# Silu evaluated on ScalarE in one group a tile, z projected a tile ahead, convolution taps folded into the projection's weights

## What is computed

```python
def silu(v): return v * sigmoid(v)
x_d, z = split(einsum('btm,im->bti', x, W_in))       # 512 channels each
xc = depthwise causal conv of x_d, 4 taps, + conv_b
x_d = silu(xc)
ssm_in = x_d @ W_x.T                                  # dt_raw (1), B (16), C (16)
delta = softplus(dt_raw * W_dt + b_dt)
for each token:                                       # the scan, h is [512, 16]
    h = exp(delta * A) * h + delta * B * x_d
    y = (h * C).sum(over the 16 states)
y = (y + D * x_d) * silu(z)
x = y @ W_out.T                                       # residual and layer norm follow
# experts: h = silu(t @ wg.T) * (t @ wu.T); out += weight * (h @ wd.T)
```

## Time and profile before

| | |
|---|---|
| time, median of 3 runs | 1134.51 us (1130.51 to 1134.89) |
| the profiled execution | 1135.04 us, its span 1133.2 us |
| busy share of the span | PE 85%, DVE 82%, POOL 70%, PEld 64%, ACT 60% |
| mean granted TensorE clock | 0.949 |
| start, to the first scan | 46.4 us |
| mixer stage, 11 tiles | 46.4 to 774 us |
| between the stages | 774 to 801 us |
| expert stage | 801 to about 1105 us, then the last sums to 1133 us |

### The profile page before, as it was taken

How to read it: one execution, slowest core, us unless ns; L and a number is a source line. 1 busy time by engine, 2 the same in 40 slices (tenths; PEclk the granted TensorE clock), 3 DMA queues, 4 the chain that set the end, 5 groups by cost and what they waited for, 6 DMA issues and landing times.

```text
span 1133.2 us, 16674 instructions
## 1 busy us (share of the span) xinstructions
PE 964.0 (85%) x4563; PEld 725.6 (64%) x4563; DVE 928.9 (82%) x1821; ACT 681.6 (60%) x1802; POOL 788.1 (70%) x839
## 2 busy tenths in 40 slices
PE   5698889988798888989978896866599999999990
PEld 5575666656566566666756663534388888878880
DVE  3589999999999999999999999896244677767774
ACT  3685675757567575666757657541266666666661
POOL 2244478878788787888878888787501676767775
PEclk8999999999999999999999999878799999999996
DMA  4599500201111020111202010058566898889883
GB/s 150 176 327 325 160 24 24 62 15 59 38 50 52 19 80 18 54 42 33 74 15 59 10 53 29 28 210 354 146 188 179 251 269 263 260 259 277 265 265 108
DMA packets 104474, 149.21 MB, mean 132 GB/s; under 512 B 14111, under 2 KB 91359, under 8 KB 104127
## 3 DMA queue, kind: packets, MB, share of 16 engines
q1 hardware_dynamic: 87487, 106.35, 29.3%
q0 software_dynamic: 16896, 41.80, 13.0%
HBM read 71.28 MB, written 76.82 MB: 131 GB/s over the span
## 4 chain that ended last, share of the span: by engine, by line
POOL 26%; PE 26%; issue 18%; DVE 17%; ACT 7%; DMA 3%; SPq 1%; POOLq 0%; DVEq 0%; ACTq 0%
POOL arena L630 11%; PE BC L1007 11%; DVE arena L1408 9%; POOL pool_dram L618 6%; PE Y L1001 3%; PE F L1021 3%; PE K L1021 3%; DMA mixer_own<-pool_dram 3%; DVE arena L1420 2%; ACT D L1118 2%; PE Y L842 2%; POOL arena L637 1%; PE D L1013 1%; ACT arena L1069 1%; POOL gat L686 1%
## 5 line engine op out<-in xcount | busy, mean ns | idle before, releaser
L1408 DVE TENSOR_TENSOR_SCAN arena<-D,arena 128x444 f32<-128x444 f32 (+1 forms) x352 | 351.1, 1037 | 12.4 <-ACT D L1118 8.3
L842 PE MATMUL Y<-arena,ident 128*128 128x444 f32 (+1 forms) x704 | 303.3, 559 | 1.6 <-DVE arena L1420 1.6
L686 POOL DMA_INDIRECT gat<-y_dram,slot_all x176 | 173.5, 986 | 127.5 <-DMA y_dram<-mixer_own 72.5
L618 POOL DMA_INDIRECT pool_dram<-hrow,slot_of x176 | 175.4, 997 | 45.3 <-issue 38.1
L630 POOL TENSOR_TENSOR arena<-mixer_own,arena 128x888 f32<-128x888 f32 (+1 forms) x90 | 163.9, 1823 | 53.2 <-ACT arena L1106 51.6
L1118 ACT ACTIVATE D<-mixer_own,aneg 128x216 f32<-128x216 f32 (+1 forms) x384 | 148.5, 427 | 82.4 <-DVE arena L1408 82.2
L1420 DVE TENSOR_TENSOR arena<-arena,BC 128x888 f32<-128x888 f32 (+1 forms) x176 | 184.8, 1050 | 5.4
L1007 PE MATMUL BC<-arena,xt 128*128 x716 | 185.3, 382 | 0.0
L630 POOL TENSOR_TENSOR arena<-arena 128x888 f32<-128x888 f32 x75 | 143.4, 1913 | 53.8 <-ACT arena L1106 52.9
L842 PEld LDWEIGHTS Y<-arena,ident 128*128 128x128 f32 x704 | 127.0, 199 | 74.8 <-issue 70.0
L1118 ACT ACTIVATE D<-arena,aneg 128x216 f32<-128x216 f32 x320 | 126.8, 437 | 73.1 <-DVE arena L1408 73.1
(11 more groups left out here) (232 smaller groups left out, 1644.1 us busy)
## 6 DMA issues: line engine op xcount, KB each, us to landing
mixer_own<-pool_dram SPq DMA_DIRECT2D x179, 144.0 KB, 3.6
y_dram<-mixer_own SPq DMA_DIRECT2D x179, 128.0 KB
pool_dram<-filler SPq DMA_DIRECT2D x5, 4176.0 KB, 31.4
arena<-in_experts_dram SPq DMA_DIRECT2D x1, 7680.0 KB, 22.8
arena<-in_x_dram SPq DMA_DIRECT2D x10, 648.0 KB, 4.0
pool_dram<-filler SPq DMA_DIRECT2D x1, 4896.0 KB, 36.1
arena<-in_experts_dram SPq DMA_DIRECT2D x1, 4608.0 KB, 17.5
pool_dram<-hrow,slot_of POOLq DMA_INDIRECT x176, 2.7
```

What stands on the lines that cost most here:

```text
L618: nc.gpsimd.indirect_dma_start(out=pool_rows, out_offset=bass.IndirectOffsetOnAxis(ap=slot_of[q][0:r, b, k:k + 1], axis=0), in_=hrow[q][0: ...
L686: nc.gpsimd.indirect_dma_start(out=gat[0:r, k, b, :], out_offset=None, in_=y_rows[0:(blocks_by(t) - k) * P, :], in_offset=bass.IndirectOff ...
L842: mm = nc.tensor.matmul(Y[j][:, 0:w], ident[:], read[g % 3][:, j * w:(j + 1) * w], start=(s == 0), stop=(s == STATES - 1), skip_group_chec ...
L1408: nc.vector.tensor_tensor_scan(state[g % 2][:, lo:hi], D[b][:, 0:hi - lo], drive[g % DRIVES][:, lo:hi], 0.0, ALU.mult, ALU.add).then_inc(s ...
```

## The change

- **Silu on ScalarE.** The function Silu is evaluated directly. `take_conv` (step 1) copies the first half of the convolution raw into x2, `silu_conv` (step 8) evaluates the second half out of bank F and the first half in SBUF. `silu_z` (step 8) evaluates all of z, 888 elements. The shared expert's gate moves to step 8. The set with Ln and exp is loaded again right behind this group. VectorE's four products of 444 a tile and one of the two of `shared_expert` and of `hidden` are gone.
- **z a tile ahead.** `project_z` now takes tile n = i+1 in steps 12 and 14, and ScalarE copies it to `z_raw` (`take_z`). It took tile i before. `add_tokens` waits for `z_taken` instead of VectorE's last product.
- **Taps in the weights.** `inw4` holds the projection's weights times each tap (set up once by VectorE, 8 products of 512 elements). `convolve(n, c, k)` multiplies the tokens themselves: 32 + 4 matmuls a tile, and no `project_x`, no `copy_x_d`. The tap weights are loaded broadcast over the 128 partitions.
- **Softplus moved.** `softplus_small` goes from step 13 to step 12, `softplus_large` from behind the read-out of step 13 to ahead of it. `shared_expert` goes from the end of step 8 to between scan and read-out of step 9.

```diff
-inw_x = carve(KM * DI).rearrange("p (k d) -> p k d", k=KM)
-diag_w = carve(KI * TAPS * P).rearrange("p (c a d) -> p c a d", c=KI, a=TAPS)
-x_d = carve(2 * N)
+inw4 = carve(KM * TAPS * DI).rearrange("p (k a d) -> p k a d", k=KM, a=TAPS)
 xw = carve(KI * SPLIT).rearrange("p (c a r) -> p c a r", c=KI, a=3)
 dtw = carve(KI * P).rearrange("p (c d) -> p c d", c=KI)
-half_tanh, soft, small, series = (carve(KI * N) for _ in range(4))
+logs, soft, small, series = (carve(KI * N) for _ in range(4))
...
+inw_x = arena[:, at_drive:at_drive + KM * DI].rearrange("p (k d) -> p k d", k=KM)
+convw = arena[:, at_drive + 2 * KI * N:at_drive + 2 * KI * N + TAPS * DI].rearrange("p (a d) -> p a d", a=TAPS)
...
-tanh_z, z2, gated, delta_even, du_even = (mixer_own[:, n] for n in range(5))
+z_raw, z2, gated, delta_even, du_even = (mixer_own[:, n] for n in range(5))
...
-CONV_LOADS = [(inw_x, w_in_x), (convw[:], conv_w),
+CONV_LOADS = [(inw_x, w_in_x), (convw, conv_w.broadcast_to([P, TAPS, DI])),
...
-    def project_x(n, b):
-
-        if b == 0:
+    def convolve(n, c, k):
+        if c == 0 and k == 0:
             pe.wait_ge(h0_done, n + 1)
-        else:
-            pe.wait_ge(x2_done, 2 * n + 1)
-        if n == 0:
-            pe.wait_ge(conv_in, 16 * len(CONV_LOADS))
+        if n == 0 and c == 0:
+            pe.wait_ge(inw4_done, k + 1)
+        if c == 2 and k == 0:
+            pe.wait_ge(conv_taken, n + 1)
         w = width(n)
-        for c in range(2):
-            for k in range(KM):
-                at = 2 * b + c
...
+        to = F[:, (c % 2) * w:(c % 2 + 1) * w]
         for back in range(TAPS):
-            nc.tensor.matmul(to.rearrange("p (a t) -> p a t", t=TOKENS)[:, :, back:], diag_w[:, c, TAPS - 1 - back, :],
-                             of[:, :, 0:TOKENS - back], start=(back == 0), stop=False, skip_group_check=True)
-        if n == 0 and c == 0:
...
+            nc.tensor.matmul(to.rearrange("p (a t) -> p a t", t=TOKENS)[:, :, back:], inw4[:, k, TAPS - 1 - back, c * P:(c + 1) * P],
+                             h0[n % 3][:, k, 0:images(n), 0:TOKENS - back], start=(k == 0 and back == 0), stop=False,
+                             skip_group_check=True)
+        if k == KM - 1:
+            if n == 0 and c == 0:
+                pe.wait_ge(bias_split, 4)
+                pe.wait_ge(one_rows_step, 4)
+            nc.tensor.matmul(to, bias_rows[:, c * P:(c + 1) * P], one_rows[:, 0:w], start=False,
+                             stop=True, skip_group_check=True).then_inc(conv_done, 1)
...
-    def project_z(i, b):
+    def project_z(n, b):
+
         if b == 1:
-            pe.wait_ge(z2_done, 2 * i + 1)
+            pe.wait_ge(z_taken, 2 * n + 1)
         else:
-            if i > 0:
-                pe.wait_ge(rank_taken, i)
-            else:
+            if n > 1:
+                pe.wait_ge(rank_taken, n - 1)
+            if n == 0:
                 pe.wait_ge(mixer_in, 16 * len(MIXER_LOADS))
-            if i + 1 < TILES:
-                pe.wait_ge(bc_split, SPLITS * (i + 1) + 2)
-        w = width(i)
+            pe.wait_ge(bc_split, SPLITS * n + 2)
+        w = width(n)
...
-        pe.wait_ge(z2_done, 2 * t + 2)
+        if t + 1 < TILES:
+            pe.wait_ge(z_taken, 2 * t + 4)
+        else:
+            pe.wait_ge(rank_taken, t)
...
-            convolve(n, 1)
+            for k in range(KM):
+                convolve(n, 1, k)
...
-        if front and s == 4:
-            project_x(n, 1)
-        if front and s == 6:
-            convolve(n, 2)
+        if front and s in (4, 5):
+            convolve(n, 2, s - 4)
...
-        if front and s == 8:
-            convolve(n, 3)
+        if front and s in (7, 8):
+            convolve(n, 3, s - 7)
...
-        if mix and s in (12, 14):
-            project_z(i, (s - 12) // 2)
+        if front and s in (12, 14):
+            project_z(n, (s - 12) // 2)
         if i + 2 < TILES:
             if s in (11, 13):
                 project_patches(i + 2, (s - 11) // 2)
-            if s == 14:
-                project_x(i + 2, 0)
-            if s == 15:
-                convolve(i + 2, 0)
+            if s in (14, 15):
+                convolve(i + 2, 0, s - 14)
...
-    def copy_x_d(n, b):
-        act.wait_ge(x_d_done, 2 * n + b + 1)
-        if 2 * n + b > 0:
...
+    def take_conv(n):
+
+        act.wait_ge(conv_done, KI * n + 2)
+        if n > 1:
+            act.wait_ge(x_added, n - 1)
+            act.wait_ge(du_done, n - 1)
+        nc.scalar.activation(cut(x2[n % 2], n)[:, 0:2, :], pair(F, n), ACT.Copy).then_inc(conv_taken, 1)
+
+    def silu_conv(n):
+        act.wait_ge(conv_done, KI * n + 4)
+        nc.scalar.activation(cut(x2[n % 2], n)[:, 2:4, :], pair(F, n), ACT.Silu).then_inc(x2_done, 1)
+        act.wait_ge(conv_taken, n + 1)
+        nc.scalar.activation(cut(x2[n % 2], n)[:, 0:2, :], cut(x2[n % 2], n)[:, 0:2, :], ACT.Silu).then_inc(x2_done, 1)
+
+    def take_z(n, b):
+        act.wait_ge(z_done, 2 * n + b + 1)
         if n > 0:
-            act.wait_ge(x2_done, 2 * (n - 1) + b + 1)
-            act.wait_ge(soft_sum, n)
-        nc.scalar.activation(cut(half_tanh, n)[:, 2 * b:2 * b + 2, :], pair(F, n), ACT.Tanh, scale=0.5).then_inc(conv_tanh, 1)
...
+            act.wait_ge(z2_done, n)
+        nc.scalar.activation(cut(z_raw, n)[:, 2 * b:2 * b + 2, :], pair(K, n), ACT.Copy).then_inc(z_taken, 1)
+
+    def silu_z(i):
+        act.wait_ge(z_taken, 2 * i + 2)
         if i > 0:
-            act.wait_ge(z2_done, 2 * (i - 1) + b + 1)
-        nc.scalar.activation(cut(tanh_z, i)[:, 2 * b:2 * b + 2, :], pair(K, i), ACT.Tanh, scale=0.5).then_inc(z_tanh, 1)
+            act.wait_ge(gated_done, 2 * i)
+        nc.scalar.activation(cut(z2, i), cut(z_raw, i), ACT.Silu).then_inc(z2_done, 1)
...
-            act.wait_ge(shared_act, t)
-        nc.scalar.activation(tanh_s[:, 0:width(t)], K[:, 0:width(t)], ACT.Tanh, scale=0.5).then_inc(shared_tanh, 1)
+            act.wait_ge(shared_hid, t)
+        nc.scalar.activation(silu_s[:, 0:width(t)], K[:, 0:width(t)], ACT.Silu).then_inc(shared_silu, 1)
...
         if front and s == 1:
-            tanh_conv(n, 0)
-        if front and s == 5:
-            copy_x_d(n, 1)
+            take_conv(n)
         if back and s == 5:
             normalise(t)
         if back and s == 6:
             copy_h1t(t)
         if back and s == 7:
             logit_exp(t)
-        if back and s == (7 if mix else 9):
+        if back and s == (8 if mix else 9):
             shared_gate(t)
         if front and s == 8:
-            tanh_conv(n, 1)
+            silu_conv(n)
+        if mix and s == 8:
+            silu_z(i)
+        if mix and s == 8:
+            nc.scalar.preload_act_table_set("natural_log_exp_and_others")
...
-        if mix and s in (12, 14):
-            tanh_gate(i, (s - 12) // 2)
-        if i + 2 < TILES and s == 14:
-            copy_x_d(i + 2, 0)
+        if front and s == 14:
+            take_z(n, 1)
         if back and s == (13 if front else 11):
             weights(t)
         if front and s == 12:
             if mix:
                 copy_b(STATES * i + s + 3)
-            nc.scalar.preload_act_table_set("natural_log_exp_and_others")
             softplus_ln(n)
             softplus_series(n)
-
-    copy_x_d(0, 0)
+            take_z(n, 0)
...
-    def set_up_taps():
+    def set_up_conv(k):
         dve.wait_ge(conv_in, 16 * len(CONV_LOADS))
-        dve.wait_ge(ident_step, 2)
-        for c in range(KI):
-            for a in range(TAPS):
-                last = nc.vector.tensor_scalar(diag_w[:, c, a, :], ident[:], convw[:, c, a:a + 1], None, ALU.mult)
-        last.then_inc(taps_done, 1)
+        for a in range(TAPS):
+            last = nc.vector.tensor_tensor(inw4[:, k, a, :], inw_x[:, k, :], convw[:, a, :], ALU.mult)
+        last.then_inc(inw4_done, 1)
...
-    def silu_conv(n, b):
-        dve.wait_ge(conv_tanh, 2 * n + b + 1)
-        if n > 1:
...
-        nc.vector.scalar_tensor_tensor(cut(du[n % 2], n), cut(x2[n % 2], n), 0.5, cut(delta[n % 2], n), ALU.mult,
-                                       ALU.mult).then_inc(du_done, 1)
+        dve.wait_ge(x2_done, 2 * n + 2)
+        nc.vector.tensor_tensor(cut(du[n % 2], n), cut(x2[n % 2], n), cut(delta[n % 2], n), ALU.mult).then_inc(du_done, 1)
...
-    def silu_z(i, b):
-        dve.wait_ge(z_tanh, 2 * i + b + 1)
-        nc.vector.scalar_tensor_tensor(cut(z2, i)[:, 2 * b:2 * b + 2, :], cut(tanh_z, i)[:, 2 * b:2 * b + 2, :], 1.0,
-                                       pair(K, i), ALU.add, ALU.mult).then_inc(z2_done, 1)
-
     def gate(t):
-        dve.wait_ge(z2_done, 2 * t + 2)
+        dve.wait_ge(z2_done, t + 1)
         dve.wait_ge(y_added, STATES * (t + 1))
         if t > 0:
             dve.wait_ge(mixed, 2 * t)
         for b in range(2):
-            nc.vector.scalar_tensor_tensor(cut(gated, t)[:, 2 * b:2 * b + 2, :], pair(Y[b], t), 0.5,
```

(31 more changed lines are left out.)

80 lines of the change are left out of this document (25 added, 55 removed).

## The result

The changed kernel takes 1155.2 us (median of 4, 1153.8 to 1157.7) against 1134.7 for the kernel before on the same chip: 1.0185 times as long, 95% interval 1.0147 to 1.0223. The forecast was 1104, the range 1088 to 1123. The profiled execution has a span of 1156.0 us against 1133.2.

A forecast was written before the change was run, and what follows sets the result against it. VectorE was taken to bound the mixer tiles and TensorE the expert stage. Savings on VectorE less waits, collisions and start costs summed to -29.7 us from 1135.0, giving 1105; it said 1104 by 65.0 us tiles, range 1088 to 1123.

The forecast's parts named there:

- The part on ScalarE's step 8: ScalarE's silu group with two table loads takes 4.9 us; `copy_b` and state 10's decays behind it just fit, stall 0.
- the part on GpSimd: VectorE wants GpSimd's softplus product 4.7 us earlier, GpSimd manages 3.05, margin 0.8: wait 0.85 us a tile, bounds 0 and 2.0.
- The router's term: VectorE's small router instructions can be hit by GpSimd's drives: 0.5 us lost a tile, bounds 0 and 4.
- (c): On VectorE, `softplus_large` starts ahead of GpSimd's drive and falls from 2.81 to 1.14 us: 1.67 saved, 0 if they meet.
- The rival named for the slower side: Router instructions of steps 8 to 10 meet drives, 4.1 us a tile, `softplus_large` stays 2.8: about 1143 us, chance 5%.
- Tile 0: Narrow first tile: 3.1 us of stall from ScalarE's group against 2.8 us removed; taken as +1, bounds -2 and +4.
- The start: Before the first scan: broadcast tap loads, eight weight products, more matmuls and table loads; +2.5 us, bounds 0 and +7.
- (a): Four VectorE products of 444 leave each tile, 0.53 us each, 2.12 us for four.
- (b): One of the shared expert's two products leaves VectorE in each tile, 0.41 us.
- the clock drop of step 1: TensorE runs at half clock after waiting 3.44 us for the read-out; expected gone, 1.7 us back on TensorE.
- the row of Ln: Profile row on ScalarE: Ln starts 0.01 us behind a 1.28 us table load, so no 1.38 us drain was priced.
- The expert stage: TensorE-bound stage after the mixer tiles: blocks as before, one product less saving 0.3 us once.

The follow-up runs named there:

- accum_forms: Changed kernel with `gmask`, `chosen` and `softplus_small` in the form that also writes their sum; period 69.9 us, 1.008 times the kernel before.
- copyb_early: Changed kernel with ScalarE's copy of B for step 11 moved ahead of z's silu; period 66.7 us, 0.984 times the kernel before.
- pe_order: Changed kernel with the first half of the convolution's last chunk moved from TensorE's step 7 to step 8; period 69.7 us, 1.007 times the kernel before.
- ko_before: Kernel before with GpSimd's 15 drives a tile replaced by writes of zeros; period 68.2 us, 0.993 times the kernel before.
- copyb_scatters_pe: Changed kernel with the early copy of B, two GpSimd scatters moved behind its product, the convolution's last chunk whole in step 8; period 64.6 us, 0.980 times before.
- best_again: The same kernel as copyb_scatters_pe, run again on a chip with the usual expert stage; 1107.9 us, 0.976 times the kernel before.

## Why the prediction was wrong

**What failed.** The part on ScalarE's step 8. It named what waits behind the silu group, `copy_b` and the decays of state 10, and priced only the decays: "It just fits: stall 0". That half holds: the group took 4.7 us from 333.89 to 338.56, and before `chosen` no scan waits. But `copy_b` has another reader, GpSimd, and its idle time there, 2.21 us, stands in no term. In the part on GpSimd I let it be 3.05 us earlier and had VectorE wait 4.7 - 3.05 - 0.8 = 0.85 us. With the 2.21 taken off that it is 3.06, and accum_forms, where nothing is stretched, measured 3.0. copyb_early, where the copy comes 2.3 us sooner after the group's first load, left a wait of 1.15, near the 0.85 forecast.

The mechanism was right and the missing wait decided it, but that the figures agree so well is luck in part. Drive 6 starts 1.7 us sooner after the gate (13.6 for 15.3), near the 1.9 forecast. From there to the product the kernel before takes 40.9 us and the forecast had 39.8, with 1.1 us of stretch gone; copyb_early takes 41.1, with a new wait of 0.84 us for the row B of state 10 in it (pe_order, which puts TensorE's half chunk of step 7 back, has no such wait). Counted from the gate the product ends at 56.8 us there where the forecast's working gives 55.0, and VectorE is ready for it at 55.8 where that gives 54.2: both sides were off, and the difference was not. And a wait of 3.06 us would by the forecast's own terms make a tile of 66.7 us (65.0 less 0.85 and 0.5, and 3.06), where accum_forms has 69.9: 1.6 us of that are decays, 0.6 the gate, 0.5 the slower form of `softplus_small`, and some 0.5 I do not place.

**The router's term.** 0.5 us a tile with bounds 0 and 4; measured 3.9 for `gmask`, `chosen` and `wsel`, and 2.0 for `softplus_small`, which had no term though it too reads and writes SBUF alone. With (c) that is 7.1 us a tile over the forecast, against 0.85 of wait that did not occur; the tile came out 5.5 over it, so some 0.8 of gain elsewhere is not placed. I took meetings as chance hits. They are not: an engine that has met another starts level with it. The rival named for the slower side was this one, with 4.1 us and `softplus_large` unchanged, at 1143 and a chance of 5%. Its form was right, its price was too low (2.0 us a tile lost where it had 0.9) and its cause was missing.

**Term (c).** `softplus_large` stayed at 2.83 us where I had 1.14. I compared its new start with the drive's old one and left the drive where it was. Both come later together (53.48 and 53.45 us after the gate, where they had 52.32 and 52.25). The term itself came true where the meetings ahead of it were gone: `softplus_large` lasts 1.12 to 1.24 us in accum_forms and 1.21 in copyb_early.

**Tile 0.** +1 forecast with bounds -2 and +4, measured +5.0. VectorE's waits for the decays in it are 6.5 us, the longest 3.2 behind the silu group, which is the estimate of 3.1; what I missed are 1.6 us for decays that stand behind the copy of the row B of state 3, which the spreading gives behind eight matmuls of the convolution in a row (16 records), and 1.7 for Ln. VectorE's waits from 45.6 to 99.9 us:

```profile
DVE arena L1387 <- ACT D L1107: 6.5, 6, 3.2
DVE arena L1355 <- ACT arena L1087: 1.7, 1, 1.7
```

**The start.** +2.5 forecast, -0.8 measured; the first scan came at 43 to 46 us in all kernels with the change.

**What held.** Terms (a) and (b): VectorE has seven instructions less in that stretch. The pair without drives differs by 4.1 us a tile: 2.5 are these products and 1.6 the wait for decays that ko_before has, and the small differences left cancel; (c) is not in it, since `softplus_large` is short in both. TensorE never became the bound, and the clock drop of step 1 is gone (the eight records behind the wait take 3.16 us, from 309.66, where they took 4.86). The table load is followed at once by the next activation, as the row of Ln had it: 337.28 + 1.28 is 338.56, and the copy starts at 338.58. By the rule of a drain behind it (the Trainium skill, ScalarE: Activation LUTs, What ACT_TABLE_LOAD costs) the group would have been 2.8 us longer, an estimate from its figure; the trace does not agree. A period of 65.0 us was forecast; with the copy, the scatters and TensorE's chunk in place it is 64.6. The expert stage was forecast to stay: from the last gate to the end takes 359.2 us before and 363.1 after, but 359.6 and 362.0 in two variants of the kernel before and 358.4 to 362.8 in variants of the changed one. That scatter is as large as the 3.8 us, and I have no cause for it.

## What to carry to other kernels

When a burst of work goes onto an engine, price everything queued behind it by each of its readers, not only by the reader that sets the pace; a copy of 0.36 us behind 4.7 us of silu cost 3.8 us a tile. Where two engines exclude each other, an instruction's stretch tells where they meet and not what can be won: take the meetings away in one run and look at which wait stands there instead. And when one engine is relieved, compare its new times with the new times of the others, since both shift.

## What the hardware showed beside it

- A VectorE instruction of 64 elements takes 1.97 us when GpSimd's drive of 1.93 us is in its way, and the same operation that also writes its sum takes 0.22 when it starts 0.1 to 0.3 us behind such a drive (accum_forms, at 546.32 and 617.13 us). The Trainium skill (SBUF — State Buffer, on the shared port pair) says so of that form, and the trace agrees. It has a price: `softplus_small` goes from 0.60 to 1.08 us.
- Who starts first is not decided by the recorded starts when they are close: `softplus_small` recorded 0.19 us ahead of the drive lost to it in the changed kernel (353.01 and 353.20, 2.59 us), and in copyb_early it won with the same 0.19 us ahead (344.13 and 344.32, 0.62 us, the drive 2.21).
- TensorE's clock after the same wait in the same kernel, at tile 0: copyb_scatters_pe waits 2.66 us ahead of a run of 16 records (eight matmuls) and runs them at full clock, granted 1.00 from 42 to 50 us; best_again, the same kernel on another chip, waits 2.65 us and gets 0.57 there, with 0.50 from 44 to 48.

```profile
42.83 3.15 PE L742 MATMUL F<-h,arena 128*128 128x222 f32 x16 [2.66 <-DVE h L1302]
```

```profile
43.41 6.05 PE L742 MATMUL F<-h,arena 128*128 128x222 f32 x16 [2.65 <-DVE h L1302]
```

  With the 6.05 us for 3.15, best_again has its first gate at 103.6 us and copyb_scatters_pe at 100.0. The changed kernel waited 1.59 us there, ran at full clock and had it at 99.95. The length of the wait alone does not decide it, and what does stays open.
